# A fused eight-stage kernel: six edits joined, in the controller of the last network, both early attentions, the third network and the last attention's prologue

## The reference, cut to what matters

```python
x = x + _L0_xattn_ref(_layernorm(x), ctx, Wq, bq, Wk, bk, Wv, bv, Wo, bo)   # attn0: windows of 16 positions along the 512
x = x + _L0_ffn_ref(_layernorm(x), gate_w, expert_w)                        # ffn0: 8 experts, the 2 best are mixed
x = x + _L1_xattn_ref(_layernorm(x), ctx, ctx)                              # attn1: softmax(k) v, then softmax(q) times it
x = x + _L1_ffn_ref(...)                                                    # ffn1: shared network and a latent path
x = x + _L2_xattn_ref(...)                                                  # attn2: 32 heads, 8 groups, rotary positions
x = x + _L2_ffn_ref(...)                                                    # ffn2: dense product, masked by cluster hits
x = x + _L3_xattn_ref(...)                                                  # attn3: 16 heads, 4 states each
x = x + _L3_ffn_ref(_layernorm(x), c1_w, c2_w, w1, w2t)                     # ffn3: a controller picks 1 of 32 hidden units
```

## Time and profile before

| | |
|---|---|
| median of 3 runs | 1727.52 us (1721.11 to 1728.83) |
| the profiled execution: its own time | 1726.33 us |
| its span | 1725.0 us |
| PE busy | 1609.3 us, 93% of the span, 9612 instructions |
| PEld, DVE, POOL, ACT busy | 1170.5, 991.9, 582.5, 470.1 us |
| mean granted clock of PE | 0.971 of full speed |

### The profile page before, as it was taken

How to read it: one execution, slowest core, us unless ns; L and a number is a source line. 1 busy time by engine, 2 the same in 40 slices (tenths; PEclk the granted TensorE clock), 3 DMA queues, 4 the chain that set the end, 5 groups by cost and what they waited for, 6 DMA issues and landing times.

```text
span 1725.0 us, 22712 instructions
## 1 busy us (share of the span) xinstructions
PE 1609.3 (93%) x9612; PEld 1170.5 (68%) x9612; DVE 991.9 (58%) x1332; ACT 470.1 (27%) x682; POOL 582.5 (34%) x406
## 2 busy tenths in 40 slices
PE   7988979999789999999999999998899998879998
PEld 2264548888458878778787787877664466558886
DVE  5976754224452666455564555545551399667665
ACT  4130011000531233343232432323112356521110
POOL 3939732221344333143231432311050244532211
PEclk9988979999899999999999999999899999989999
DMA  3000031100300211101011010100301022400000
GB/s 124 1 1 1 1 147 50 49 1 0 129 13 0 86 49 50 37 25 37 25 62 37 25 37 25 37 1 1 148 1 24 1 52 63 151 1 13 13 6 19
DMA packets 18021, 66.58 MB, mean 39 GB/s; under 512 B 1440, under 2 KB 9760, under 8 KB 13312
## 3 DMA queue, kind: packets, MB, share of 16 engines
q1 hardware_dynamic: 17920, 65.12, 10.9%
HBM read 58.82 MB, written 2.10 MB: 35 GB/s over the span
## 4 chain that ended last, share of the span: by engine, by line
PE 76%; DVE 13%; POOL 4%; ACT 3%; issue 2%; DMA 1%; SPq 0%; DVEq 0%; ACTq 0%; POOLq 0%
PE banks L270 46%; PE banks L264 26%; DVE arena L451 2%; PE banks L1923 1%; PE banks L408 1%; DVE arena L234 1%; POOL w_lo L2396 1%; DVE arena L1462 1%; DVE grouped_split L1494 1%; PE banks L2192 1%; PE banks L1348 1%; DVE window L499 1%; DVE arena L1449 1%; ACT arena L1562 1%; ACT arena L1561 1%
## 5 line engine op out<-in xcount | busy, mean ns | idle before, releaser
L270 PE MATMUL banks<-grouped_split 128*128 128x512 f32 x1536 | 367.6, 395 | 6.8 <-DVE grouped_split L1494 6.1
L270 PEld LDWEIGHTS banks<-grouped_split 128*128 128x128 f32 x1536 | 284.8, 189 | 70.1 <-DVE grouped_split L1494 9.3
L1628 POOL TENSOR_TENSOR arena<-arena,attn_tables 128x512 f32<-128x512 f32 x80 | 102.1, 1280 | 312.7 <-ACT arena L1562 312.7
L270 PE MATMUL banks<-experts_split 128*128 128x512 f32 (+1 forms) x792 | 181.6, 392 | 2.1 <-DVE experts_split L661 2.1
L270 PEld LDWEIGHTS banks<-experts_split 128*128 128x128 f32 (+1 forms) x792 | 146.5, 185 | 36.5 <-issue 2.4
L264 PE MATMUL banks<-arena 128*128 128x64 f32 (+2 forms) x738 | 141.7, 342 | 18.8 <-DVE arena L1462 6.8
L264 PEld LDWEIGHTS banks<-arena 128*128 128x128 f32 x738 | 103.5, 196 | 51.5 <-issue 37.6
L1449 DVE TENSOR_TENSOR arena<-banks,attn_tables 128x512 f32<-128x512 f32 x80 | 54.7, 684 | 129.9 <-ACT arena L1562 129.9
L689 DVE SCALAR_TENSOR_TENSOR arena<-banks,experts,arena 128x512 f32<-128x512 f32 x64 | 47.8, 751 | 111.3 <-PE banks L270 111.3
L1462 DVE TENSOR_TENSOR arena<-arena 128x512 f32<-128x512 f32 x80 | 70.4, 880 | 54.5 <-POOL arena L1628 54.4
L264 PE MATMUL banks<-dense 128*32 128x64 f32 (+4 forms) x1738 | 86.2, 293 | 12.2 <-DVE dense L1756 4.3
(11 more groups left out here) (295 smaller groups left out, 3054.3 us busy)
## 6 DMA issues: line engine op xcount, KB each, us to landing
grouped<-in_attn SPq DMA_DIRECT2D x16, 1024.0 KB, 5.0
experts<-in_expert SPq DMA_DIRECT2D x8, 1024.0 KB, 4.8
linear<-in_ffn SPq DMA_DIRECT2D x1, 4096.0 KB, 14.8
grouped<-in_attn SPq DMA_DIRECT2D x8, 512.0 KB, 3.5
dense<-arena SPq DMA_DIRECT2D x16, 256.0 KB, 4.6
dense<-in_w SPq DMA_DIRECT2D x1, 3584.0 KB, 12.6
dense<-in_attn SPq DMA_DIRECT2D x1, 3072.0 KB, 12.5
dense<-in_w SPq DMA_DIRECT2D x1, 2688.0 KB, 10.3
```

Of the source, the lines that this page charges most:

```text
L270: s = pe.matmul(dst, lhsT=lhsT[i], rhs=rhs[j], start=(k == 0 and x == 0), stop=(k == n - 1 and x == 2))
L1628: g_.tensor_tensor(rot, rot, SIN[:, h * HALF:(h + 1) * HALF], ALU.mult).then_inc(rot_sin.sem, 1)
```

## The change

Six edits are made together.

1. attn0: no halves. All four cuts are divided and split by DVE before the wide loop starts (`low_done(4)`); POOL only adds pairs. A unit is four 32-row products of 512 columns in place of eight of 256; a quarter is two tiles of 512 columns in place of four half tiles. `stay_busy` there is 22 products in place of 10.
2. ffn0 and attn1: the maxima of the context (DVE) and attn1's exponentials of the keys (ACT) are made in ffn0, beside the products of expert 0. `latent1` is loaded as soon as the last expert is split. attn1's PE program starts with the transposes of `ke`, and the weight product stands behind the query sums.
3. attn2: in the last group each `output_add` is followed by its tile's measurement, which stood at the head of ffn2.
4. ffn2: dense tiles 0 and 1 stand ahead of the counts, and tile 2 ahead of the row mask; the bias of the next tile is added ahead of the mask of this one.
5. attn3: the folds use banks 4 to 7 and wait no longer for the last dense tile's reader; keys and transposes alternate; ACT copies the transposes before it makes the first keys, and makes the exponentials of unit 1 ahead of the last queries.
6. ffn3: the controller goes by halves; the first half, `hidden(1)` and the first two `inter` come ahead of the transposes of tiles 4 to 7, which have buffers of their own (`XNS`). POOL makes 10 pieces of w2's low part ahead of the second reciprocal root, and 4 later.

```diff
-        stay_busy(m, pe, 4, 10)
+        stay_busy(m, pe, 7, 22)
         pe.wait_ge(*selt_done(1))
-        pe.wait_ge(*sum_done(2))
-        pe.wait_ge(*low_v(2))
+        pe.wait_ge(*low_done(4))
...
-            half, q, w = n // (2 * WIN), n // WIN % 2, n % WIN
+            p, w = n // WIN, n % WIN
             if n >= 2:
                 pe.wait_ge(*av_done(n - 1))
-            if n == 2 * WIN:
...
-            for i in range(2):
-                for x, part in enumerate((hi, lo)):
-                    for j in range(2):
-                        t = 4 * q + 2 * j + i
-                        rows = slice(t // 2 * 32, t // 2 * 32 + 32)
-                        s = pe.matmul(bank[:, n % 2 * 2 + j, i * CUT:(i + 1) * CUT], lhsT=seltr[rows, t * P:(t + 1) * P],
-                                      rhs=part[rows, w, half * CUT:(half + 1) * CUT], start=x == 0, stop=x == 1)
+            for x, part in enumerate((hi, lo)):
+                for i, t in enumerate(PAIRS[p]):
+                    rows = slice(t // 2 * 32, t // 2 * 32 + 32)
+                    s = pe.matmul(bank[:, n % 2 * 2 + i, :], lhsT=seltr[rows, t * P:(t + 1) * P], rhs=part[rows, w, :],
+                                  start=x == 0, stop=x == 1)
...
-        for c in range(2):
-            inverse(c)
+            v.reciprocal(f(SUM, D)[:, cuts[c]], bank[:, c, 0:P]).then_inc(sum_done.sem, 1)
             v.wait_ge(*sum_done(c + 1))
-            v.tensor_tensor(dots[:, :, cuts[c]], dots[:, :, cuts[c]], over_w(SUM, cuts[c]), ALU.mult).then_inc(att_v.sem, 1)
-        for c in range(2):
+            v.tensor_tensor(dots[:, :, cuts[c]], dots[:, :, cuts[c]], over_w(SUM, cuts[c]), ALU.mult).then_inc(att_done.sem, 1)
+
+        def low(c):
             v.wait_ge(*hi_done(c + 1))
             v.tensor_tensor(lo[:, :, cuts[c]], dots[:, :, cuts[c]], hi[:, :, cuts[c]].bitcast(F32),
-                            ALU.subtract).then_inc(low_v.sem, 1)
-        inverse(2)
-        inverse(3)
+                            ALU.subtract).then_inc(low_done.sem, 1)
+
+        divide(0)
+        for c in range(1, 4):
+            divide(c)
+            low(c - 1)
+        low(3)
...
-        def divide(c):
-            g.wait_ge(*sum_done(c + 1))
-            g.tensor_tensor(dots[:, :, cuts[c]], dots[:, :, cuts[c]], over_w(SUM, cuts[c]), ALU.mult).then_inc(att_g.sem, 1)
-
...
-            if k == 1:
-                divide(2)
-            if k == 5:
-                divide(3)
-            if k == 8:
-                low(2)
-            if k == 12:
-                low(3)
-            if k == 28:
+            g.tensor_tensor(f(at, 2 * D), f(at, 2 * D), f(at + 2 * D, 2 * D), ALU.add).then_inc(pair_done.sem, 1)
+            if k == 27:
                 m.rsqrt_half(g, 1, 0)
...
         v.tensor_tensor(f(WREP, 64, E0, NT), pick[0], pick[1], ALU.add).then_inc(wrep_done.sem, 1)
+        for t in range(NT):
+            v.tensor_reduce(f(NMAX1 + t, 1), f(C + t * D, D), axis=AX, op=ALU.max, negate=True).then_inc(m.nmax_done.sem, 1)
         v.wait_ge(*wrep_done(1))
         for e in range(E0):
             for t in range(NT):
@@ -712,7 +683,13 @@
         gate_rows(m, act, gate_mm, 0, rows_done, XN)
         act.wait_ge(*gap_done(1))
         act.activation(f(TMP, NT), f(TMP, NT), ACT.Exp).then_inc(frac_done.sem, 1)
-        for e in range(1, E0):
+        high(1)
+        act.wait_ge(*gate_turned(1))
+        for t in range(NT):
+            act.wait_ge(*m.nmax_done(t + 1))
+            act.activation(f(KE + t * D, D), f(C + t * D, D), ACT.Exp, bias=f(NMAX1 + t, 1),
+                           accum_out=f(KSUM1 + t, 1)).then_inc(m.ke_done.sem, 1)
+        for e in range(2, E0):
...
     def sync(sp):
+        sp.wait_ge(*m.staged_free)
+        m.load(sp, LAT, dram["latent1"], lat_in)
         sp.wait_ge(*start)
-        m.load(sp, LAT, dram["latent1"], lat_in)
         m.load(sp, UP, dram["ffn1"], f1_in)
 
     def tensor(pe):
-        pe.wait_ge(*start)
+        for t in range(NT):
+            pe.wait_ge(*ke_done(t + 1))
+            if t >= 2:
+                pe.wait_ge(*ket_out(t - 1))
+            else:
+                pe.wait_ge(*read[t])
+            turn4(m, pe, t % 2, f(KE + t * D, D)).then_inc(ket_mm.sem, 1)
+        pe.wait_ge(*m.ct_in(16))
+        pe.wait_ge(*ket_out(NT))
+        for t in range(NT):
+            if t >= 2:
+                pe.wait_ge(*kv_done(t - 1))
+            else:
+                pe.wait_ge(*read[2 + t])
+            for c in range(DC):
+                s = mm(pe, bank[:, 2 + t % 2, 0:P], f(KET + c * N + t * P, P), f(CT + c * N + t * P, P), c, DC)
+            s.then_inc(kv_mm.sem, 1)
...
         pe.wait_ge(*lat_in(16))
         for j in range(NL):
...
             v.wait_ge(*use_mm(at_use[u] + 1))
             v.tensor_tensor(x, bank[:, place(u), :], x, ALU.add).then_inc(bank_v.sem, 1)
+            if g + 1 == G2:
+                v.wait_ge(*bank_v(at_vector[u] + 1))
+                m.moments(v, 5, 4 * h + t)
...
+        dense(0)
+        dense(1)
+        pe.wait_ge(*hit_done(1))
+        for t in range(NT):
+            s = mm(pe, bank[0:NCL, 6, 0:1], f(DT + t * NCL, NCL), f(ONES, 1), t, NT)
+        s.then_inc(count_mm.sem, 1)
+        dense(2)
+        pe.wait_ge(*csel_done(1))
+        pe.wait_ge(*ahot_done(1))
+        mm(pe, bank[:, 5, :], f(QSEL + 32, P)[0:NCL, :], f(AHOT, D)[0:NCL, :]).then_inc(rsel_mm.sem, 1)
+        for t in range(3, NT):
+            dense(t)
+
...
+        with_bias(0)
+        for t in range(NT):
+            if t + 1 < NT:
+                with_bias(t + 1)
+            x = f(X + t * D, D)
             v.wait_ge(*sel_done(t + 1))
-            v.scalar_tensor_tensor(x, y, f(QSEL + t, 1), x, ALU.mult, ALU.add).then_inc(x_done.sem, 1)
+            v.scalar_tensor_tensor(x, f(YS[t % 2], D), f(QSEL + t, 1), x, ALU.mult, ALU.add).then_inc(x_done.sem, 1)
...
-                    to, mix = bank[:, n % 4, T * P:(T + 1) * P], f(MIX + T * P, P)
+                    to, mix = bank[:, 4 + n % 4, T * P:(T + 1) * P], f(MIX + T * P, P)
...
-        pe.wait_ge(*fold_out(12))
+        pe.wait_ge(*m.y_read)
...
+            if t % 4 == 3:
+                pe.wait_ge(*vn_out(t // 4 + 1))
+                k_rows(0, t // 4, t // 4, range(DC))
...
+        pe.wait_ge(*m.xt_done(32 + 4))
         q_rows(0)
+        pe.wait_ge(*m.xt_done(32 + NT))
         q_rows(1)
...
-        first_keys(0)
-        first_keys(1)
         for t in range(NT):
             act.wait_ge(*m.turned(32 + t + 1))
             act.activation(f(XT, DC * N, DC, N)[:, :, t * P:(t + 1) * P], bank[:, 2 + t % 6, :].rearrange(
                 "p (c n) -> p c n", c=DC), ACT.Copy).then_inc(m.xt_done.sem, 1)
+        first_keys(0)
+        first_keys(1)
...
             if j == 0:
                 queries(6)
-                queries(7)
             if j + 1 < NU:
                 exps(j + 1)
+            if j == 0:
+                queries(7)
...
+
+        def controller(h):
+            for c in range(DC):
+                s = mm3(pe, bank[0:96, 7 * h, :], [x[:, c * 96:(c + 1) * 96] for x in c1s],
+                        [x[:, c, h * HALF:(h + 1) * HALF] for x in xs], c, DC)
+            s.then_inc(low_mm.sem, 1)
+
         pe.wait_ge(*xlo(1))
         pe.wait_ge(*w1_lo(DC))
         pe.wait_ge(*wo_add(NT - 1))
         hidden(0)
+        pe.wait_ge(*xlo(4))
+        pe.wait_ge(*c1_lo(1))
+        controller(0)
+        pe.wait_ge(*wo_add(NT))
+        hidden(1)
+        pe.wait_ge(*c2_lo(1))
+        pe.wait_ge(*low_lo(1))
+        inter(0)
+        inter(1)
         for t in range(4, NT):
             turn_x(t)
         pe.wait_ge(*xlo(NT))
-        pe.wait_ge(*wo_add(NT))
-        pe.wait_ge(*c1_lo(1))
-        for h in range(2):
-            for c in range(DC):
-                s = mm3(pe, bank[0:96, h, :], [x[:, c * 96:(c + 1) * 96] for x in c1s],
-                        [x[:, c, h * HALF:(h + 1) * HALF] for x in xs], c, DC)
-            s.then_inc(low_mm.sem, 1)
-        hidden(1)
-        pe.wait_ge(*c2_lo(1))
-        pe.wait_ge(*low_lo(2))
-        inter(0)
-        inter(1)
+        controller(1)
...
+        v.wait_ge(*c2_lo(1))
+        low_part(0)
         pick(0)
+        for t in range(4, NT):
+            x_low(t)
+        mask(0)
         pick(1)
-        mask(0)
...
             h_low(u - 2)
+            if u == 2:
+                low_part(1)
...
+        act.activation(c2h[32:64, :], f(C2, INTER)[32:64, :], ACT.Copy).then_inc(c2_hi.sem, 1)
         w2_high(3)
+
+        def low_high(h):
+            act.wait_ge(*low_mm(h + 1))
+            cut = slice(h * HALF, (h + 1) * HALF)
+            act.activation(low[0:64, cut], bank[0:64, 7 * h, :], ACT.Copy)
+            act.activation(lowh[64:96, cut], bank[64:96, 7 * h, :], ACT.Copy).then_inc(low_hi.sem, 1)
+
+        low_high(0)
...
-        for k in range(12):
+        for k in range(10):
             w2_low(k)
         m.rsqrt_half(g, 7, 1)
-        w2_low(12)
-        w2_low(13)
...
```

(3 more changed lines are left out.)

177 lines of the change are left out of this document (67 added, 110 removed).

## The result

The changed kernel takes 1678.16 us (median of 4 runs, 1676.1 to 1682.93), the kernel before in the same rounds 1725.45: ratio 0.9732, 95% interval 0.971 to 0.9754, that is 47 us less. The forecast of 1676 lies 2 us off and the time is inside 1661 to 1690. The profiled execution of the changed kernel was the slowest of its four (1682.93, span 1681.6), 43.4 shorter than the span before.

What follows compares the result with a forecast made beforehand. PE bounds the kernel, so edits pay where it waits or runs at half clock behind a wait. Terms -3.7 - 11.8 - 23.0 - 13.1 = -51.6 from 1726.33 give 1674.7, stated as 1676 us, range 1661 to 1690.

Steps and rivals of the forecast that it cites:

- A: attn0: later loop start, against shorter wide rounds and no POOL divides or low parts in the loop; -3.7 us.
- C: attn2's end to attn3's loop: PE's waits covered or removed, folds and first scores earlier; -23.0 us.
- B: attn1: key transposes no longer wait for the load and weight product, less POOL's late root; -11.8 us.
- D: ffn3's prologue: first turn_h earlier, mask wait closed, less one possible clock fall; -13.1 us.
- Rounds of 512 columns should take 0.26: attn0's wide loop: four rounds take 1.04 us instead of 1.14, -0.10 on each of 29 pairs, -2.9 us.
- The three falls of 8.2: attn0's wide loop: one clock fall allowed behind each of three adds, 8.2 us together.
- The first unit pair and start-up: attn0's wide loop: its opening stretch in the undisturbed loop time, put at 6.9 us.
- (3): attn2's end to attn3's loop: folds start at dense's end, -13.7 us at their start, -16.1 at their end.
- Gains given back: Rival: fixed order makes a later engine late in attn0, attn1 and ffn3; 1690 to 1697 us, chance 0.14.
- Wide products that don't overlap: Rival in attn0's loop: +21 us in place of -2.9; 1697 to 1700 us, chance 0.06.
- No clock falls in attn0: Rival: attn0's loop has no clock falls; 1655 to 1662 us, chance 0.07.
- A loop all at half clock: Rival: PE stays at 1.2 GHz through attn0's whole wide loop, +77 us; 1751 us, chance 0.01.

Runs made afterwards that it cites:

- serial_wide: Changed kernel with attn0's wide-product loops over parts and tiles swapped, so one tile's high and low products stand together; 1677.86 us, ratio 0.9734.
- undo_attn0: Changed kernel with attn0 as in the kernel before; 1680.04 us, ratio 0.9744.
- undo_attn1: Changed kernel with ffn0 and attn1 as in the kernel before; 1697.00 us, ratio 0.9828.
- one_group: Changed kernel with all eight wide products of a pair of units on the same 32 rows, for timing only (output not the reference's); 1694.92 us in one run.

## Why the prediction was right, and where it was not

**The whole** was right by the mechanism that it named in attn1, ffn2, attn3 and ffn3, which carry the gain; A's gain isn't told from none. A and C were forecast too large, by 2 and by 4 to 5, and B and D lie within what was measured (10.9 to 12.8 for 11.8, 12.3 to 15.5 for 13.1). That the forecast is only 2 off is in part luck: 51.5 less than 1727.52 was forecast and 47.3 less was measured, but against a kernel before that took 1725.45 in these rounds.

**A, -3.7 forecast, -1.9 by the undone part.** The start (+7.3) came as worked out, 119.73 for 119.4. *"Rounds of 512 columns should take 0.26"* failed: a pair's eight products take 1.13 us and took 1.14, so the price goes by columns, 0.28 ns each for 32 rows on two groups, and there is no overhead of a round to save: 0.5 where 2.9 were booked. The Trainium skill ("TensorE: Matmul & The Clock Gate", section "The mechanism") lets a weight load overlap a running product only if their row groups differ. By that rule the prediction had 1.18 for the eight; the trace is nearer to that than to its 1.04, but `serial_wide`, in which every second product follows one of its own group, is no slower, so the rule as I used it isn't what sets the 1.13. PE's wait for an add is 1.07 + 0.40 = 1.47, not 2.0. The three falls of 8.2 were 1.7 + 1.7 + 5.1 in the changed kernel's profiled execution and 1.7 + 1.7 + 0 in most others. The first unit pair and start-up, booked at 6.9, took 10.3 to 10.7, half clock included, and 10.36 before the change: the sum took 3.5 us away there that the change doesn't touch. With 121.86 us in `undo_attn0` and 128.18 in the kernel before for the same code, the sign of A isn't settled: at ffn0 the undone kernel is at 234.24, those with the change at 235.5 to 240.9.

**B, -11.8.** `widen` came 12.6 earlier against the last expert (431.36 before, 432.07 now), with nothing of the product sticking out. POOL's root was late as forecast, its low parts of the weights ending at 471.6 for "about 471"; PE's wait behind it grew by 3.1 (1.63 to 4.72) for the 1.9 booked, and that wait is one of the signs that the prediction named for being wrong. One price was missing: the clock was at half behind the 4.72. It cost nothing up to the first gate product (8.9 us from the first transpose to it, before and after) and 1.4 in the gate products (gate1 to groups, 134.86 for 133.45). ffn0 to gate1 gives 10.9 from the two profiled kernels and 12.8 from `undo_attn1`.

**C, -23.0.** 16.2 to the first score and 2.9 from there to hidden, 19.1; 18.3 by the medians of the undone part, and 21.5 by its column, in which the fall in ffn2 is counted that neither the kernel before nor the changed one had in their profiled executions. Against the start of attn2's last group (8.77 earlier than before) dense ends at 1263.8 of the old time for 1263.6, and turns, keys and queries took 17.3 for 17.5. The mis-sized term is (3): *"their 18.22 us held another 1.7 of half clock, and what is left, 0.7, is their waiting for ACT's copies"*. The clock was half there, but the folds running in it were those that take as long at either clock, and the biases now wait for the twelfth copy (0.69), a wait that the change added. The end of the folds came 12.6 earlier and not 16.1. Behind it the clock fell in the first value products (29.22 us for 27.65). The last exponentials gave 1.8, as booked.

**D, -13.1.** The undone part gives 12.3, the column 13.3 to 15.5. `turn_h(0)` stands at 1530.1 of the time before (shifted by the 27.9 gained up to there) for 1530.6. The clock fall allowed for, 1.5, did not come.

**The rivals.** Gains given back: in B by POOL's root and the clock, 1 to 2 us of the 17 that it needed. Wide products that don't overlap: `one_group` shows the price, 20, and that it wasn't paid. No clock falls in attn0: each profiled execution had them. A loop all at half clock: the stretches ended by themselves each time.
